# Query norms by matmuls into a column of ones, key scales in another instruction form, and a new order of the engines' work in a fused attention and expert kernel

## The chip, the cores and the metric

The kernel runs on one core of a Trainium2 chip. The metric is the device time of one execution in microseconds; the median of three runs is given, and one further execution was profiled. The engines named below are PE (TensorE; its weight loads have rows of their own, PEld), ACT (ScalarE), DVE (VectorE), POOL (GpSimd) and SP, which issues most transfers. Each has its own stream of instructions, executed in program order, and waits on semaphores of the others.

## The reference, cut to what matters

The whole is a two-layer block: linear attention with a gated delta rule (32 value heads, 16 key heads) beside 64 routed experts, then a small second layer. The change lies in the first layer's attention:

```python
mixed = hidden_states @ w_qkv
y = conv1d(x, conv_w, groups=CONV_DIM)             # 4 taps per channel
mixed = silu(y)
q, k, v = jnp.split(mixed, [KEY_DIM, 2 * KEY_DIM], axis=-1)
q = q / sqrt(sum(q * q, axis=-1) + 1e-6) * DK ** (-0.5)
k = k / sqrt(sum(k * k, axis=-1) + 1e-6)
# over the tokens: S = S * exp(g); delta = (v - k S) * beta; S = S + k^T delta; o = q S
og = o * silu(z)
on = og * rsqrt(mean(og * og) + EPS) * norm_w
out = on.reshape(B, S, VAL_DIM) @ w_out
```

Here the sum of `q * q` over the 128 channels of a head is what the change computes in another way.

## The kernel before, in words

The attention and the experts run together in `heads_and_experts`, in 64 steps g: 16 key heads by four chunks of 128 tokens, for all four batches at once. The chunk of a step is c = g mod 4; c = 0 is the first chunk of a head and c = 3 the last. The work is a pipeline of three steps' depth: step g projects, convolves and squares the keys, queries and values of chunk g, inverts the triangular matrices of chunk g-1, and solves, updates the state and writes the output of chunk g-2. So `state_update`, which is left out in a head's last chunk, is left out in the steps with c = 1. What each engine does in a step is written out by hand in five functions called `step`, one for each engine; this order is what decides who waits.

Keys and queries come out of the convolution with channels on the partitions and tokens along the row. To sum squares over channels, the kernel before turned them on PE (`turn_keys` and `turn_queries`, line 822: four transposes each into a PSUM bank), and ACT squared the turned tile with an accumulated row sum (`squares`, line 1166: four ACTIVATEs and four reads of the accumulator). The turned keys are needed anyway (`keys_copy`, line 1172); the turned queries served the sums alone. The PSUM banks `psF0` and `psF1` are used in turn by 16 places in a fixed order (`PLACES`), even places in one bank and odd ones in the other; a place may be filled when the place two before it has been drained (`slot_free`). Two of these hold for the steps that follow: `EX_IN` (the turned expert input) waits for ACT's `values(g-1, 0)` (line 1189), and `PRODUCTS1` waits for the drain of `QUERIES_T`.

After the queries come `products` on PE (line 844: keys by keys and queries, half 0 and half 1), which DVE scales into `ATP` (`decayed_products`, line 1461). Between the halves stands `state_update(g-2, 0)` (line 962), which waits for POOL's `rho_w` (line 1726), and this for `gated` (line 1743) and DVE's `outputs` (lines 1528 and 1531). DVE's `key_scales` (lines 1440 to 1442) makes from the keys' square sums the scales `sj` that `decayed_products` needs. `conv` is line 1417, `decays` line 1451, `normed` on POOL line 1749, the `join` of the triangular inverse on POOL lines 1710 to 1716, `history` on DVE line 1432 (1434 for a head's first chunk). In steps with c = 3, DVE rounds the next head's weights in three parts (`high_part`, line 574), and POOL computes the remainder of each (`low_part`, line 578) and has `hidden` (line 1757) and `mask` (line 1695) in its queue between them.

## Time and profile before

| what | before |
|---|---|
| median of 3 runs | 2678.14 us (2676.47 to 2680.68) |
| the profiled execution, its own time | 2679.44 us |
| its span, first to last instruction | 2677.7 us |
| mean granted clock of TensorE | 0.958 of full speed |
| PE busy | 2362.6 us (88%) |
| DVE busy | 2326.0 us (87%) |
| ACT busy | 1788.2 us (67%) |
| POOL busy | 1424.9 us (53%) |

A share of busy time is a mean over the span. The 64 steps begin at about 106 us and end near 2300 us; before them stands the setup, behind them the second layer. A row of the timeline gives the start, the duration, the engine, the line of the kernel and what was written and read; in brackets is how long the engine had sat idle before, and whose work ended that.

### The profile page before, as it was taken

How to read it: one execution, taken by the hardware profiler on the slowest of the kernel's cores; microseconds unless marked ns; L12 is line 12 of the kernel's file. 1: busy time of each engine (PE TensorE's matmuls, PEld its weight loads, DVE VectorE, ACT ScalarE, POOL GpSimd, SP SyncE). 2: the span in 40 equal slices, each digit the busy share in tenths (PEclk: the TensorE clock that was granted, in tenths of full speed). 3: DMA queues.
4: the chain of work that ended last, by engine and by line, in shares of the span. 5: the costliest groups of instructions: out<-in, count | busy, mean ns of one | idle time of the engine just before them, and what ended most of it. 6: DMA issues, size and time to landing. Idle time of an engine off the chain costs nothing. (4 is left out here: it accounts for less than half of the span.)

```text
span 2677.7 us, 74015 instructions
## 1 busy us (share of the span) xinstructions
PE 2362.6 (88%) x27695; PEld 1951.4 (73%) x27696; DVE 2326.0 (87%) x5305; ACT 1788.2 (67%) x5621; POOL 1424.9 (53%) x1368
## 2 busy tenths in 40 slices
PE   1477889999999999999999999999999999758998
PEld 1366777888787878787878787878787878635555
DVE  7677888999999999999999999999999998289996
ACT  1356767787878787878787878787877787412121
POOL 2388885555555555555555555555555555266510
PEclk8679899999999999999999999999999999869999
DMA  5232112212222222221222222212122112263311
GB/s 208 89 94 67 41 42 61 57 50 51 55 57 50 57 50 57 49 57 49 57 50 57 50 57 50 57 49 58 49 57 49 46 49 57 64 206 106 104 59 48
DMA packets 244701, 175.39 MB, mean 66 GB/s; under 512 B 152635, under 2 KB 212714, under 8 KB 243160
## 3 DMA queue, kind: packets, MB, share of 16 engines
q1 hardware_dynamic: 221543, 136.89, 19.1%
q0 software_dynamic: 12288, 24.19, 2.9%
q10 hardware_dynamic: 10512, 9.57, 1.1%
q8 instruction: 222, 3.64, 0.6%
q14 instruction: 136, 1.11, 0.1%
HBM read 126.88 MB, written 53.08 MB: 67 GB/s over the span
## 5 line engine op out<-in xcount | busy, mean ns | idle before, releaser
L1417 DVE SCALAR_TENSOR_TENSOR p_y<-p_xr,cw,p_y 128x512 f32<-128x512 f32 x768 | 760.3, 997 | 33.2 <-ACT p_y L1141 14.4
L798 PE MATMUL p_psF<-xnS,w_hl 128*128 128x512 f32 x1536 | 430.6, 416 | 20.4 <-PEq L651 11.1
L798 PEld LDWEIGHTS p_psF<-xnS,w_hl 128*128 128x128 f32 x1536 | 274.4, 192 | 85.9 <-DVE p_ATP L1461 11.4
L1710 POOL TENSOR_TENSOR p_terms<-p_U 64x512 f32<-64x512 f32 x64 | 130.8, 2043 | 335.8 <-DVE p_U L1486 335.7
L1461 DVE SCALAR_TENSOR_TENSOR p_ATP<-p_psF,p_sj,p_E 128x256 f32<-128x256 f32 x512 | 211.0, 477 | 65.8 <-PE p_psF L844 64.2
L1749 POOL TENSOR_TENSOR p_O<-p_OG,p_sm 128x512 f32<-128x512 f32 x128 | 155.7, 1239 | 195.0 <-DVE p_sm L60 171.8
L1743 POOL TENSOR_TENSOR p_OG<-p_O,p_zs 128x512 f32<-128x512 f32 x128 | 162.6, 1271 | 140.5 <-ACT p_ktok L1172 69.3
L979 PE MATMUL p_psO<-p_wout,p_ont 128*128 128x256 f32 x1024 | 235.3, 383 | 0.1
L1712 POOL TENSOR_TENSOR p_terms<-p_terms 64x256 f32<-64x256 f32 (+1 forms) x256 | 220.0, 859 | 20.1
L1138 ACT ACTIVATE p_xr<-p_psF 128x512 f32<-128x512 f32 x256 | 153.4, 599 | 93.6 <-PE p_psF L798 81.8
L813 PEld LDWEIGHTS p_psF<-w_hl,xnS 128*128 128x128 f32 x1536 | 200.1, 189 | 14.3 <-DVE p_ATP L1461 5.1
L979 PEld LDWEIGHTS p_psO<-p_wout,p_ont 128*128 128x128 f32 x1024 | 191.4, 192 | 25.2 <-ACT p_ont L1253 0.8
L1246 ACT ACTIVATE p_O<-p_OG 128x128 f32<-128x128 f32 x512 | 152.4, 308 | 82.4 <-POOL p_OG L1743 81.7
L813 PE MATMUL p_psF<-w_hl,xnS 128*128 128x256 f32 x1536 | 206.0, 284 | 0.0
L1141 ACT ACTIVATE p_y<-p_psF,cw 128x512 f32<-128x512 f32 x256 | 175.0, 684 | 0.8
L1166 ACT ACTIVATE p_y<-p_psF 128x128 f32<-128x128 f32 x512 | 137.1, 300 | 48.2 <-PE p_psF L822 48.2
L822 PE MATMUL p_psF<-ident,p_kq 128*128 128x128 f32 x512 | 86.1, 292 | 93.7 <-ACT p_kq L1151 93.5
L1451 DVE TENSOR_TENSOR_SCAN p_E<-p_ab,p_identr 128x512 f32<-128x512 f32 x128 | 160.6, 1255 | 8.2 <-DMA p_ab<-decays 8.2
L1966 POOL DMA_INDIRECT w_hl<-expert_out,slot_u x96 | 100.8, 1050 | 86.9 <-DVE acc L2211 36.2
L1189 ACT ACTIVATE p_vs<-p_psF,p_vsc 128x128 f32<-128x128 f32 x512 | 146.2, 379 | 0.0
L822 PEld LDWEIGHTS p_psF<-ident,p_kq 128*128 128x128 f32 x512 | 54.8, 143 | 124.1 <-ACT p_kq L1151 124.1
L844 PE MATMUL p_psF<-p_kq 128*128 128x256 f32 x512 | 138.1, 395 | 5.5 <-ACT p_y L1166 5.5
(337 smaller groups left out, 6153.8 us busy)
## 6 DMA issues: line engine op xcount, KB each, us to landing
p_ab<-decays SPq DMA_DIRECT2D x64, 512.0 KB, 5.5
w_raw<-in_w_in SPq DMA_DIRECT2D x16, 768.0 KB, 4.0
p_wgu<-in_w_gu SPq DMA_DIRECT2D x60, 176.0 KB
expert_out<-p_ye ACTq DMA_DIRECT2D x73, 128.0 KB, 1.7
expert_in<-p_zero SPq DMA_DIRECT2D x16, 512.0 KB, 7.5
blocks_out<-p_ATc SPq DMA_DIRECT2D x64, 128.0 KB
p_DTc<-blocks_back SPq DMA_DIRECT2D x64, 128.0 KB
p_xe<-expert_in SPq DMA_DIRECT2D x60, 128.0 KB
```

The source lines that it names most:

```text
L798: m = pe.matmul(b4(psF[f % 2][:, :]), w_hl[:, wp, kt, ty * P:(ty + 1) * P], xnS[:, xp, kt, :].rearrange("p (b t) -> p b t", b=B)[:, :, c * ...
L813: m = pe.matmul(psF[f % 2][:, (b % 2) * 2 * P:(b % 2 + 1) * 2 * P], xnS[:, xp, kt, b * S + c * P:b * S + (c + 1) * P], w_hl[:, wp, kt, 4 * ...
L979: m = pe.matmul(psOO[:, b * D:(b + 1) * D], ont[:, v, b, :], wout[:, v, :], start=(v == 0), stop=(v == 1))
L1138: act.activation(xr[:, ty, :, TAPS - 1:], b4(psF[f % 2][:, :]), ACT.Copy)
L1141: act.activation(y[:, ty, :, :], b4(psF[f % 2][:, :]), ACT.Copy, scale=cw[:, ty, TAPS - 1:TAPS]).then_inc(s["drained"], 1)
L1246: m = act.activation(O1[:, v, b, :], OG[:, v, b, :], ACT.Square, accum_out=so[:, v, b:b + 1])
L1417: m = dve.scalar_tensor_tensor(y[:, ty, :, :], xr[:, ty, :, tap:tap + P], cw[:, ty, tap:tap + 1], y[:, ty, :, :], ALU.mult, ALU.add)
L1451: dve.tensor_tensor_scan(flat(E[:, v, :, :]), flat(ab[:, v, :, :]), flat(identr[:, :, :]), 0.0, ALU.mult, ALU.add).then_inc(s["scan"], 1)
L1461: m = dve.scalar_tensor_tensor(ATP[g % 2][:, v, b, :, :], psF[f % 2][:, (b % 2) * 2 * P:(b % 2 + 1) * 2 * P].rearrange("p (u t) -> p u t", ...
L1712: link(pool.tensor_tensor(terms[:, 0:k, :, :], terms[:, 0:k, :, :], terms[:, k:2 * k, :, :], ALU.add))
L1743: pool.tensor_tensor(OG[:, v, :, :], O1[:, v, :, :], zs[g % 2][:, v, :, :], ALU.mult).then_inc(s["og"], 1)
L1749: pool.tensor_tensor(O1[:, v, :, :], OG[:, v, :, :], over(sm[:, 1, 1 + v, :]), ALU.mult).then_inc(s["on"], 1)
```

## The change

The sums of the queries' squares take another way. ACT squares the queries where they lie (`query_squares`, one ACTIVATE of 128x512 into `y`), PE multiplies each batch's 128x128 squares by a column of ones (`query_norms`, four matmuls with one moving column), and ACT copies the four resulting columns (`query_sums`). The turning of the queries and their four accumulating squares go. In `key_scales` the addition of 1e-6 and the product with the gates become SCALAR_TENSOR_TENSOR instructions; the first now reads a second tensor, `floor`, in place of an immediate. The rest is order: on PE, `EX_IN` goes between the two halves of `within`, and `EX_UP` ahead of `level_y`; on ACT, `silu` of the queries goes ahead of `keys_copy`, and `evacuate(g, 2)` ahead of `inverse_copy`; on DVE, `decays(g, 1)` goes ahead of `pivots`, `history(g-1, 1)` behind `conv(g, 0)`, and `output_weights` and the first part of the next weights between the two last convolutions.

```diff
             @block.vector
-                for t in (xr[:, :, :, 0:TAPS - 1], scratch[:, :], D64X[:, :, :, :], TT[0][:, :, :, :]):
+                for t in (xr[:, :, :, 0:TAPS - 1], D64X[:, :, :, :], TT[0][:, :, :, :]):
                     dve.memset(t, 0.0).then_inc(init, 1)
+                dve.memset(ones[:, :], 1.0).then_inc(init, 1)
+                dve.memset(floor[:, :], 1e-6).then_inc(init, 1)
...
-            def turn_queries(g):
-                wait(pe, "silu", g, 2)
-                turn(g, QUERIES_T, lambda b: kq[g % 2][:, b, Q_, :])
+            def query_norms(g):
+
+                slot_free(g, QUERIES_T)
+                wait(pe, "squared", g, 1)
+                for b in range(B):
+                    m = pe.matmul(psF[QUERIES_T % 2][:, b:b + 1], y[:, 1, b, :], ones[:, :], start=True, stop=True)
+                m.then_inc(s["filled"], 1)
...
@@ PE, step @@
                     within(g - 2, 0)
+                expert(g, EX_IN)
+                if g >= 2:
                     within(g - 2, 1)
-                expert(g, EX_IN)
-                turn_queries(g)
+                query_norms(g)
                 products(g, 0)
...
+                expert(g, EX_UP)
                 if g >= 1:
                     level_y(g - 1, 4)
-                expert(g, EX_UP)
...
@@ ACT @@
-            def squares(g, u):
-
-                p, f = g % 2, (KEYS_T, QUERIES_T)[u]
-                wait_filled(act, g, f)
-                if u == 0:
-                    wait(act, "vsc", g - 2, 1)
+            def key_squares(g):
+
+                wait_filled(act, g, KEYS_T)
+                wait(act, "vsc", g - 2, 1)
                 for b in range(B):
-                    m = act.activation(y[:, u, b, :], psF[f % 2][:, b * P:(b + 1) * P], ACT.Square, accum_out=ss[p][:, u, b:b + 1])
-                m.then_inc(s["drained" if u else "kss"], 1)
+                    m = act.activation(y[:, 0, b, :], psF[KEYS_T % 2][:, b * P:(b + 1) * P], ACT.Square, accum_out=ss[g % 2][:, 0, b:b + 1])
+                m.then_inc(s["kss"], 1)
+
+            def query_squares(g):
+
+                wait(act, "silu", g, 2)
+                act.activation(y[:, 1, :, :], kq[g % 2][:, :, Q_, :], ACT.Square).then_inc(s["squared"], 1)
+
+            def query_sums(g):
+
+                wait_filled(act, g, QUERIES_T)
+                act.activation(ss[g % 2][:, 1, :], psF[QUERIES_T % 2][:, 0:B], ACT.Copy).then_inc(s["drained"], 1)
...
@@ ACT, step @@
                 if g >= 1:
                     values(g - 1, 0)
+                silu(g, 1)
                 keys_copy(g)
-                silu(g, 1)
+                query_squares(g)
                 expert(g, EX_IN)
-                squares(g, 1)
+                query_sums(g)
...
@@ DVE, key_scales @@
-                link(dve.tensor_scalar(sm[:, 0, 0, :], ss[g % 2][:, 0, :], 1e-6, None, ALU.add))
+                link(dve.scalar_tensor_tensor(sm[:, 0, 0, :], ss[g % 2][:, 0, :], 1.0, floor[:, :], ALU.mult, ALU.add))
                 link(dve.reciprocal(n2[:, :], sm[:, 0, 0, :]))
-                dve.tensor_tensor(sj[:, :, :], gates[:, 0, g % NC:NT:NC, h:h + 2], n2[:, :].unsqueeze(2).to_broadcast([P, B, 2]), ALU.mult).then_inc(s["s_ready"], 1)
+                dve.scalar_tensor_tensor(sj[:, :, :], gates[:, 0, g % NC:NT:NC, h:h + 2], 1.0, n2[:, :].unsqueeze(2).to_broadcast([P, B, 2]), ALU.mult, ALU.mult).then_inc(s["s_ready"], 1)
...
@@ DVE, step @@
+                decays(g, 1)
                 if g >= 1:
                     pivots(g - 1)
-                decays(g, 1)
                 conv(g, 0)
+                if g >= 1:
+                    history(g - 1, 1)
                 if g >= 2:
                     level6(g - 2)
                     residual(g - 2, 1)
                 conv(g, 1)
-                if g >= 1:
-                    history(g - 1, 1)
...
-                output_weights(g)
                 rows_decay(g)
                 row_scales(g)
                 conv(g, 3)
+                output_weights(g)
+                next_weights(g, 0)
                 conv(g, 2)
                 if g >= 1:
                     level(g - 1, 4)
                 next_taps(g)
-                next_weights(g, 0)
                 next_weights(g, 1)
```

PE's instructions between the solve and the products, in a step without a state update (c = 1), before (`p_psS` is the solve, `p_psO` the product within the chunk, `p_xe` the expert input, `p_kq` keys and queries):

```order
L943 MATMUL p_psS<-p_vs,p_TT 128x128 x8
L953 MATMUL p_psO<-p_Ws,p_ATP 128x128 x8
L991 MATMUL p_psF<-ident,p_xe 128x128 x2
L822 MATMUL p_psF<-ident,p_kq 128x128 x4
L844 MATMUL p_psF<-p_kq 128x256 x4
```

And of the changed kernel at the same place:

```order
L950 MATMUL p_psS<-p_vs,p_TT 128x128 x8
L960 MATMUL p_psO<-p_Ws,p_ATP 128x128 x4
L998 MATMUL p_psF<-ident,p_xe 128x128 x2
L960 MATMUL p_psO<-p_Ws,p_ATP 128x128 x4
L837 MATMUL p_psF<-p_ones,p_y 128x1 x4
L851 MATMUL p_psF<-p_kq 128x256 x4
```

The four transposes are gone, and four matmuls with one column stand in their place, ahead of the products as the transposes did.

ACT at the same place in the program, from the values of the chunk before to the output's squares, before:

```order
L1189 ACTIVATE p_vs<-p_psF,p_vsc 128x128 x4
L1172 ACTIVATE p_ktok<-p_psF 128x512
L1151 ACTIVATE p_kq<-p_y 128x4x128
L1266 ACTIVATE p_xeT<-p_psF 128x256
L1166 ACTIVATE p_y,p_ss<-p_psF 128x128 x4
L1246 ACTIVATE p_O,p_so<-p_OG 128x128 x8
```

And of the changed kernel:

```order
L1207 ACTIVATE p_vs<-p_psF,p_vsc 128x128 x4
L1161 ACTIVATE p_kq<-p_y 128x4x128
L1190 ACTIVATE p_ktok<-p_psF 128x512
L1180 ACTIVATE p_y<-p_kq 128x512
L1284 ACTIVATE p_xeT<-p_psF 128x256
L1185 ACTIVATE p_ss<-p_psF 128x4
L1264 ACTIVATE p_O,p_so<-p_OG 128x128 x8
```

The queries' squares now stand third, ahead of PE's sums; before they stood behind PE's turning.

DVE at the end of a step with c = 3, where the next head's weights are rounded, before (`p_y` from `p_xr` is the convolution, `w_hl` the rounded weights, `p_St` the state):

```order
L1417 SCALAR_TENSOR_TENSOR p_y<-p_xr,cw,p_y 128x512 x6
L1504 TENSOR_TENSOR p_Dc<-p_Dc,p_psI 128x256
L1505 STREAM_TRANSPOSE p_DTc<-p_Dc 128x256
L1601 COPY cw<-cw_raw 128x16
L574 CAST w_hl<-w_raw 128x2x256 x2
L1551 TENSOR_TENSOR p_St<-p_St,p_psS 128x512 x2
L574 CAST w_hl<-w_raw 128x2x256
L1451 SCALAR_TENSOR_TENSOR p_E<-p_ab,p_identr 128x512
```

And of the changed kernel:

```order
L1435 SCALAR_TENSOR_TENSOR p_y<-p_xr,cw,p_y 128x512 x3
L575 CAST w_hl<-w_raw 128x2x256
L1435 SCALAR_TENSOR_TENSOR p_y<-p_xr,cw,p_y 128x512 x3
L1522 TENSOR_TENSOR p_Dc<-p_Dc,p_psI 128x256
L1523 STREAM_TRANSPOSE p_DTc<-p_Dc 128x256
L1619 COPY cw<-cw_raw 128x16
L575 CAST w_hl<-w_raw 128x2x256
L1569 TENSOR_TENSOR p_St<-p_St,p_psS 128x512 x2
L575 CAST w_hl<-w_raw 128x2x256
L1469 SCALAR_TENSOR_TENSOR p_E<-p_ab,p_identr 128x512
```

The first of the three casts has moved ahead of three taps; the two others keep their places.

## Rows read from the trace of the kernel before

**Rows 1.** The page's busy time and share of the span

```profile
PE 2362.6 (88%) x27695; PEld 1951.4 (73%) x27696; DVE 2326.0 (87%) x5305; ACT 1788.2 (67%) x5621; POOL 1424.9 (53%) x1368
```

**Rows 2.** Window: length, busy and count of PE, PEld, DVE, ACT, POOL; clock; DMA

```profile
650.00:1161.00 511.00, 482.83 (x6422) 414.07 (x6421) 472.26 (x1042) 409.52 (x1312) 274.38 (x264) 1.00 0.22 54
```

**Rows 3.** Who DVE waited for, 300 to 2200 us: total, times, longest

```profile
DVE p_ATP L1461 <- PE p_psF L844: 44.4, 85, 6.5
```

**Rows 4.** Timeline of ACT in a step with c = 1

```profile
1246.16 1.14 ACT L1189 ACTIVATE p_vs<-p_psF,p_vsc 128x128 f32<-128x128 f32 x4
1247.16 0.63 ACT L1172 ACTIVATE p_ktok<-p_psF 128x512 f32<-128x512 f32 x1
1247.63 0.66 ACT L1151 ACTIVATE p_kq<-p_y 128x512 f32<-128x512 f32 x1
1249.04 0.28 ACT L1166 ACTIVATE p_y<-p_psF 128x128 f32<-128x128 f32 x1 [0.47 <-PE p_psF L822]
```

**Rows 5.** Timeline of PE in the same stretch

```profile
1248.35 0.65 PE L822 MATMUL p_psF<-ident,p_kq 128*128 128x128 f32 x4 [0.34 <-ACT p_kq L1151]
1248.84 1.03 PE L844 MATMUL p_psF<-p_kq 128*128 128x256 f32 x4
1251.62 1.65 PE L798 MATMUL p_psF<-xnS,w_hl 128*128 128x512 f32 x6 [0.25 <-DVE p_ATP L1461]
```

**Rows 6.** Timeline of DVE and POOL in the same stretch

```profile
1247.86 1.27 POOL L1743 TENSOR_TENSOR p_OG<-p_O,p_zs 128x512 f32<-128x512 f32 x1 [2.26 <-ACT p_ktok L1172]
1247.95 1.20 DVE L1442 TENSOR_TENSOR p_sj<-gates,p_n 128x8 f32<-128x8 f32 x1
1249.91 3.23 DVE L1461 SCALAR_TENSOR_TENSOR p_ATP<-p_psF,p_sj,p_E 128x256 f32<-128x256 f32 x8 [0.17 <-PE p_psF L844]
```

**Rows 7.** Timeline: sixteen matmuls with eight columns, in the second layer

```profile
2471.13 1.85 PE L2045 MATMUL p_psM<-p_rt,p_xnt 128*128 128x8 f32 x16
```

**Rows 8.** Timeline of PE in steps with c = 2, 3 and 0

```profile
1144.93 1.03 PE L844 MATMUL p_psF<-p_kq 128*128 128x256 f32 x4
1146.14 1.16 PE L962 MATMUL p_psS<-p_Wr,p_ktok 128*128 128x128 f32 x8 [0.18 <-POOL p_Wr L1726]
...
1178.53 1.03 PE L844 MATMUL p_psF<-p_kq 128*128 128x256 f32 x4
1179.87 1.16 PE L962 MATMUL p_psS<-p_Wr,p_ktok 128*128 128x128 f32 x8 [0.31 <-POOL p_Wr L1726]
...
1214.94 1.03 PE L844 MATMUL p_psF<-p_kq 128*128 128x256 f32 x4
1216.47 1.16 PE L962 MATMUL p_psS<-p_Wr,p_ktok 128*128 128x128 f32 x8 [0.50 <-POOL p_Wr L1726]
```

**Rows 9.** Timeline of DVE and POOL at the end of a step with c = 3

```profile
1193.49 1.39 POOL L578 TENSOR_TENSOR w_hl<-w_raw,w_hl 128x512 fp32r<-128x512 f32 x1 [4.84 <-DVE w_hl L574]
...
1194.86 2.63 DVE L574 CAST w_hl<-w_raw 128x512 fp32r<-128x512 f32 x1
1195.26 0.71 POOL L1695 TENSOR_TENSOR p_M<-p_ATc,masks 128x256 f32<-128x256 f32 x1
1195.94 1.26 POOL L578 TENSOR_TENSOR w_hl<-w_raw,w_hl 128x512 fp32r<-128x512 f32 x1
1197.41 1.21 DVE L1451 TENSOR_TENSOR_SCAN p_E<-p_ab,p_identr 128x512 f32<-128x512 f32 x1
```

**Rows 10.** Line 574 alone: count, duration in ns min/median/max, first and last start

```profile
L574 DVE CAST w_hl<-w_raw x45: 406/419/2636, 233.7 to 2132.9; 128x512 fp32r<-128x512 f32 x45
```

**Rows 11.** Timeline of ACT in the step behind the weights, c = 0

```profile
1207.54 0.63 ACT L1151 ACTIVATE p_kq<-p_y 128x512 f32<-128x512 f32 x1 [1.52 <-DVE p_y L1417]
```

**Rows 12.** Timeline: DVE beside POOL

```profile
1142.43 0.29 DVE L1432 COPY p_xr<-p_xr 128x24 f32<-128x24 f32 x1
...
1152.74 1.04 POOL L1749 TENSOR_TENSOR p_O<-p_OG,p_sm 128x512 f32<-128x512 f32 x1 [4.42 <-DVE p_sm L60]
1152.78 1.55 DVE L1417 SCALAR_TENSOR_TENSOR p_y<-p_xr,cw,p_y 128x512 f32<-128x512 f32 x1
```

More of the change, by code:

```diff
@@ L418 @@
 PARTS = [(kt, wp, xp) for kt in range(KT) for wp, xp in ((0, 0), (0, 1), (1, 0))]
-PER = dict(hist=2, silu=2, silu_v0=1, silu_v1=1, kss=1, vsc=1, s_ready=1, scan=2, rho=1, atp=4,
+PER = dict(hist=2, silu=2, squared=1, silu_v0=1, silu_v1=1, kss=1, vsc=1, s_ready=1, scan=2, rho=1, atp=4,
            compact=4, masked=1, halved=2, pivoted=1, joined=1, spread=4, t5=3, tt=1,
@@ L477, in heads_and_experts @@
         n2 = sb("n2", [P, B])
-        scratch = sb("scratch", [P, 1])
+        floor = sb("floor", [P, B])
+        ones = sb("ones", [P, 1])
         vsc = sb("vsc", [P, B])
@@ L653, in _ @@
             def _(dve):
-                for t in (xr[:, :, :, 0:TAPS - 1], scratch[:, :], D64X[:, :, :, :], TT[0][:, :, :, :]):
+                for t in (xr[:, :, :, 0:TAPS - 1], D64X[:, :, :, :], TT[0][:, :, :, :]):
                     dve.memset(t, 0.0).then_inc(init, 1)
+                dve.memset(ones[:, :], 1.0).then_inc(init, 1)
+                dve.memset(floor[:, :], 1e-6).then_inc(init, 1)
                 dve.tensor_copy(identr[:, :, :], ident[:, :].unsqueeze(1).to_broadcast([P, B, P])).then_inc(init, 1)
-                dve.wait_ge(init, 8)
+                dve.wait_ge(init, 9)
             @block.gpsimd
@@ L1138, in evacuate @@
                 act.activation(xr[:, ty, :, TAPS - 1:], b4(psF[f % 2][:, :]), ACT.Copy)
+                if ty == Q_:
+                    wait_filled(act, g - 1, QUERIES_T)
                 if ty >= 2:
@@ L1293, in step @@
                     queries(g - 2, 1)
-                squares(g, 0)
+                key_squares(g)
                 if g >= 2:
@@ L1310, in step @@
                 compact(g)
+                evacuate(g, 2)
                 if g >= 1:
                     inverse_copy(g - 1, 4)
-                evacuate(g, 2)
                 silu_z(g, 1)
-                if g >= 2:
-                    out_turned(g - 2, 0)
                 if g >= 1:
@@ L1319, in step @@
                 if g >= 2:
+                    out_turned(g - 2, 0)
                     out_turned(g - 2, 1)
@@ L1657, in _ @@
             pivots(STEPS - 1)
+            history(STEPS - 1, 1)
             level6(STEPS - 2)
             residual(STEPS - 2, 1)
-            history(STEPS - 1, 1)
             outputs(STEPS - 2, 0)
@@ L1797, in step @@
                 scatter(g, 9)
+                scatter(g, 10)
                 hidden(g)
                 mask(g)
-                scatter(g, 10)
                 scatter(g, 11)
@@ L1803, in step @@
                 scatter(g, 13)
+                scatter(g, 14)
                 next_weights(g, 1)
-                scatter(g, 14)
                 next_weights(g, 2)
```

## The prediction

> **What bounds the kernel now.** I read the page first: PE is busy for 88% of the span and DVE for 87%, ACT for 67%, POOL for 53% [rows 1]. In a window of the settled part they come to 482.83 and 472.26 us of 511, at full clock [rows 2]: two engines near their limit that hand work to each other, so the question is which wait ends last at the place that is changed. The list of waits says that DVE waits most for the products of line 844, 44.4 us in 85 waits [rows 3]. The timeline of one step shows how the work hangs together there (c = 1, 1246 to 1253 us). ACT is continuously at work: values at 1246.16, the keys' copy at 1247.16, silu of the queries at 1247.63, done at 1248.29 [rows 4]. PE turns the queries at 1248.35, 0.06 us behind, having waited 0.34 us, and starts the products at 1248.84 [rows 5]. DVE starts on them at 1249.91, 1.07 us later, having waited 0.17 us [rows 6]. PE's next projection starts at 1251.62, released by DVE, 0.25 us late [rows 5]. So in this stretch the chain ACT, PE, DVE, PE has no slack worth the name; what comes later on it makes the step longer. In the other three kinds of step a state update stands between the halves of the products, and PE waits before it for POOL, 0.18, 0.31 and 0.50 us [rows 8]: this is the slack there.
>
> **The queries' sums.** I count from V, the start of the values on ACT (1246.16 in rows 4). Before: keys' copy at V + 1.00, silu at V + 1.47, done at V + 2.13; turning from V + 2.19 to the products at V + 2.68. After: silu at V + 1.00, the keys' copy 0.52 later at V + 1.52 (the distance from silu to the next ACTIVATE, 1247.63 to 1248.15, which holds for any successor), the squares at V + 2.0 (a copy's distance is 0.47, from rows 4). The trace has no ACTIVATE that squares 128x512; the nearest rows are 0.63 for the copy and 0.66 for silu of the same shape [rows 4], so 0.65, done at V + 2.65, and PE 0.06 behind at V + 2.71. Taking silu out ahead of the keys' copy wins 0.47, and the extra pass loses more.
>
> The four matmuls of one column aren't in the trace either. Turning took 0.49 us for four (1248.35 to 1248.84, rows 5). The nearest row is the second layer's with 128x128 weights and eight columns: sixteen in 1.85 us [rows 7], so about 0.11 each with the tail of the last taken off. An fp32 product of 128 rows makes two such instructions in the trace (a state update with four calls is x8 [rows 8]), so eight, 0.9 us. The other bound is the spacing of the turning itself, 0.49 / 4 = 0.12, for four only if each call made one instruction: 0.5 us. I take 0.9, since rows 7 are the same kind in all but seven columns. The products then start at V + 2.71 + 0.90 = V + 3.61: **0.92 us later** than before.
>
> The Trainium skill (TensorE: Matmul & The Clock Gate, Back-to-back issue gap) puts a matmul of 1 to 64 columns at some 60 cycles, about 25 ns, in isolation. Eight would then be 0.2 us and the products only 0.2 us late. Rows 7 disagree, at 0.11 us with eight columns, and I follow them; the smaller figure is the rule's side of rival B.
>
> What the 0.92 costs in each kind of step. c = 1: products, DVE and the next projection follow without slack, **+0.92** (PE no longer waits between the halves for ACT's four squares, but DVE took both halves without a break, x8 in 3.23 us [rows 6], so that wait was hidden). In the others PE is free for the state update some 0.88 us after the products' start (they take 1.03, of which I give 0.15 to the tail of the last), and the update started when POOL was done:
> - c = 2: 1144.93 + 0.92 + 0.88 = 1146.73 against 1146.14 [rows 8], **+0.59**
> - c = 3: 1178.53 + 1.80 = 1180.33 against 1179.87, **+0.46**
> - c = 0: 1214.94 + 1.80 = 1216.74 against 1216.47, **+0.27**
>
> The second half and the projections follow the update. Together +2.24 us in four steps. `EX_IN` ahead of the second `within` costs nothing: it must wait until the values are drained at V + 1.2, takes 0.2, and 0.9 of `within` ends at V + 2.3, ahead of the squares at V + 2.71; DVE wants it no sooner, since line 1442 holds it until 1249.15 [rows 6]. If the squares came earlier, this would be late next. ACT's four accumulating squares go (from 1249.04 on [rows 4]), but the output's squares behind them start when the sums are copied, at V + 3.9, where they started before.
>
> **The scales' form.** Line 1442 took 1.20 us for eight elements, from 1247.95 to 1249.15, and POOL's `gated` ran from 1247.86 to 1249.13 [rows 6]: DVE stood until POOL was done. Does the other form escape? The convolution is of that form, and beside POOL it takes 1.55 us, ending 0.55 us behind POOL's end at 1153.78 [rows 12]. So it stands as well, and I cost the edit at nothing; bounds: 0 and 1.0 us of DVE. Even the 1.0 would be covered, as DVE then waits for the products, which come 0.92 later. The new first instruction, with its second tensor, ends before POOL starts.
> The Trainium skill (SBUF — State Buffer, Who interferes with whom) says the same against this edit: a DVE instruction with two SBUF inputs contends with a GpSimd one that reads SBUF, and the second to issue blocks fully; by that rule, as by the rows, the form is worth 0.
>
> **The weights, c = 3.** The third cast takes 2.63 us, from 1194.86, where its kind takes 0.42 in the median [rows 9, 10]: POOL has the remainder of the first part, `hidden`, `mask` and the remainder of the second in its queue, back to back until 1197.20, and DVE comes after them. With the first cast ahead of three taps, POOL's first remainder (1.39) runs beside them. I follow both queues: cast 0.42; the first tap; POOL's remainder holds the second tap by 0.75, `hidden` and the like the third by 0.10; that is 1.27 added ahead of `level`. Behind it, the two other parts with the state's sums need 2.9 us more until the scan, which comes at about 1196.35 in place of 1197.41 [rows 9]: **-1.1 us**. Bounds: 0 (each hold only moves to another instruction) and 2.2 (2.63 - 0.42, all of it). The next step, c = 0, can take it: there silu of the keys waited 1.52 us for DVE [rows 11], so up to 1.5 us count and 1.1 do.
>
> **The order's rest.** The scan ahead of `pivots`: the same instructions before `conv(g, 0)`, and POOL's `join` is held by a tap in place of the scan; 0. `history` (0.29 us beside POOL, rows 12) now delays the residual by 0.3 to 0.5 us, where the solve of that half has about that much room; 0, bound +0.4 in three of four steps. `EX_UP`, the copies and `output_weights`: 0, each has work of its engine's own before what waits for it. POOL's queue changes only in the first eight steps, one scatter a step.
>
> **The sum.** +2.24 - 1.1 = +1.1 us for four steps. For the 14 groups from step 8 on, +16 (1.14 x 14). In the first eight steps POOL's scatters stand in the same queue and lead, and I take 0. The profiled execution took 2679.4 us, so 2695.4; it lies 1.3 above the median of the runs shown, so **2694 us**.
>
> **The rivals.** A is the forecast, 2687 to 2702, chance 0.45.
> B: one column is cheap. At 0.5 us for the sums the products are 0.5 late: +0.5, +0.2, 0 and 0, less 1.1, is -0.4 us for four steps: 2672. Against it rows 7. Chance 0.12.
> C: the weights give all of the 2.2 us, the wait of ACT [rows 11] and 0.7 of DVE's own waits behind it: 2.24 - 2.2 is nothing, 2678, no change. For it the 2.63 [rows 9]; against it that POOL's work still has to run beside DVE's. Chance 0.16.
> D, the other side: the late products are absorbed, since PE gets to the projections no later than the wait for POOL allowed, for instance because rho comes late as well in most steps. It decides if the slack of 0.2 to 0.5 us [rows 8] is in truth 0.9 and more; then only the weights count, -1.1 x 14: 2663. Chance 0.12.
> E: `history` behind the first convolution stands behind POOL's `join` and delays solve, V and all behind it by 0.4 in three of four steps: 17 more (1.2 x 14), 2711. Chance 0.15.
>
> Within 0.2% (5.4 us) is what a measurement can't tell from no change. Slower: A and E, 0.60; faster: B and D, 0.24; same: C, 0.16. The range leaves out half of E and most of D: 2667 to 2711. A alone would be 2687 to 2702.
>
> **What would show it.** Right: the products start 3.6 us behind the values in every step; the eight instructions of one column take 0.9; PE waits for POOL before a state update no more; the scales' last instruction still takes 1.2 us; the third cast falls below 1 us; ACT waits 0.4 us or so in c = 0. Wrong: if the sums take under 0.5 us, if four steps together get no longer, or if the scales' product falls to 0.2 us and DVE gets ahead with it.

## The result and the profile after

| | before | after |
|---|---|---|
| median of 5 runs | 2680.57 us (2676.47 to 2682.32) | 2708.86 us (2706.32 to 2712.28) |
| ratio | 1 | 1.0111, 95% interval 1.0099 to 1.0123 |
| profiled execution: its own time, its span | 2679.44, 2677.7 us | 2708.57, 2706.8 us |
| mean granted clock | 0.958 | 0.963 |

The changed kernel is 1.1% slower, 28 us; forecast were 16. The direction and the range held, the size did not: it is nearly twice the forecast one. The page's busy times, beside [rows 1]:

```profile
PE 2387.0 (88%) x27952; PEld 1988.5 (73%) x27952; DVE 2339.8 (86%) x5306; ACT 1737.5 (64%) x5237; POOL 1386.6 (51%) x1368
```

PE works 24 us more, ACT 51 us less. That ACT has less to do brings nothing: what counts is where its new pass stands. The same window as in [rows 2] shows it in the shares:

```profile
650.00:1161.00 511.00, 480.31 (x6309) 416.43 (x6307) 464.81 (x1020) 389.11 (x1208) 263.00 (x262) 1.00 0.21 54
```

PE, DVE, ACT and POOL are all less busy in it, at full clock: each waits more. The list of waits, 300 to 2200 us (engine, line, whom it waited for: total, times, longest), names the place; beside [rows 3]:

```profile
DVE p_ATP L1479 <- PE p_psF L851: 77.0, 59, 2.3
ACT p_ss L1185 <- PE p_psF L837: 52.1, 55, 1.2
PE p_psS L969 <- POOL p_Wr L1744: 0.3, 1, 0.3
```

The last of them before:

```profile
PE p_psS L962 <- POOL p_Wr L1726: 17.3, 38, 4.4
```

DVE waits 77.0 us for the products, in place of 44.4. PE's wait for POOL ahead of the state updates, the slack of [rows 8], is down from 38 waits with 17.3 us to one of 0.3 us in the whole stretch. The timeline of ACT in a step with c = 1 answers to [rows 4]:

```profile
1395.16 1.13 ACT L1207 ACTIVATE p_vs<-p_psF,p_vsc 128x128 f32<-128x128 f32 x4
1396.16 0.66 ACT L1161 ACTIVATE p_kq<-p_y 128x512 f32<-128x512 f32 x1
1396.68 0.62 ACT L1190 ACTIVATE p_ktok<-p_psF 128x512 f32<-128x512 f32 x1
1397.15 0.66 ACT L1180 ACTIVATE p_y<-p_kq 128x512 f32<-128x512 f32 x1
1399.02 0.17 ACT L1185 ACTIVATE p_ss<-p_psF 128x4 f32<-128x4 f32 x1 [0.93 <-PE p_psF L837]
```

And PE's in the same stretch, beside [rows 5]:

```profile
1396.35 0.44 PE L998 MATMUL p_psF<-ident,p_xe 128*128 128x128 f32 x2 [0.46 <-ACT p_vs L1207]
1396.62 1.06 PE L960 MATMUL p_psO<-p_Ws,p_ATP 128*128 128x128 f32 x8
1397.96 1.02 PE L837 MATMUL p_psF<-p_ones,p_y 128*128 128x1 f32 x8 [0.28 <-ACT p_y L1180]
1398.85 1.97 PE L851 MATMUL p_psF<-p_kq 128*128 128x256 f32 x8
```

With V = 1395.16: squares done at V + 2.65, the eight column matmuls from V + 2.80, products from V + 3.69 (forecast 3.61, before 2.68). Both distances hold within 0.01 us in each of the steps 9 to 62. DVE and POOL there, beside [rows 6]:

```profile
1396.93 1.21 DVE L1460 SCALAR_TENSOR_TENSOR p_sj<-gates,p_n 128x8 f32<-128x8 f32 x1
1399.99 2.44 DVE L1479 SCALAR_TENSOR_TENSOR p_ATP<-p_psF,p_sj,p_E 128x256 f32<-128x256 f32 x6 [1.25 <-PE p_psF L851]
...
1396.85 1.27 POOL L1761 TENSOR_TENSOR p_OG<-p_O,p_zs 128x512 f32<-128x512 f32 x1 [1.95 <-DVE p_O L1549]
```

The scales' last instruction still stands until POOL is done, 1.21 us in the new form against 1.20.

ACT in the step behind the weights (c = 0), beside [rows 11], waits 0.97 us for DVE in place of 1.52 (forecast 0.4):

```profile
1492.95 0.63 ACT L1161 ACTIVATE p_kq<-p_y 128x512 f32<-128x512 f32 x1 [0.97 <-DVE p_y L1435]
```

**Step lengths.** Below, a step is measured from the start of its first scan on DVE to that of the next. The row of the scan's line gives the first and the last start of a window; four steps, 36 to 39, before and after:

```profile
L1451 DVE TENSOR_TENSOR_SCAN p_E<-p_ab,p_identr x9: 1201/1206/1396, 1333.1 to 1466.2; 128x512 f32<-128x512 f32 x9
```

```profile
L1469 DVE TENSOR_TENSOR_SCAN p_E<-p_ab,p_identr x9: 1181/1211/1218, 1347.1 to 1482.8; 128x512 f32<-128x512 f32 x9
```

133.1 and 135.7. These and the traces of the experiments give this table: the usual length of each kind of step (the value that most steps from 9 to 62 share within 0.1 us), their sum, and in how many of these 54 steps there is a stretch in which PE's loads of 128 columns take over 0.30 us in place of 0.19, that is, in which the granted clock is at the lower of its levels (1.2 GHz). The two starred lengths contain such a stretch in most steps; without it they are 33.24 and 33.49. The last column is the mean granted clock of all executions of the kernel.

| kernel | c=0 | c=1 | c=2 | c=3 | sum | steps with half clock | ratio to before, 95% | mean clock |
|---|---|---|---|---|---|---|---|---|
| before | 32.1 | 31.7 | 32.6 | 36.7 | 133.1 | 6 | 1 | 0.960 |
| after | 32.5 | 33.8 | 33.5 | 35.9 | 135.6 | 1 | 1.0111 (1.0099 to 1.0123) | 0.961 |
| a_turn | 32.1 | 32.7 | 32.9 | 35.4 | 133.1 | 1 | 0.9967 (0.9954 to 0.9981) | 0.964 |
| b_norms | 32.5 | 32.9 | 34.8* | 37.1 | 137.3 | 18 | 1.0177 (1.0153 to 1.0200) | 0.955 |
| b_weights | 32.1 | 31.7 | 32.6 | 36.2 | 132.6 | 5 | 0.9966 (0.9954 to 0.9979) | 0.962 |
| a_up_back | 32.5 | 32.9 | 35.1* | 36.7 | 137.1 | 8 | 1.0144 (1.0127 to 1.0161) | 0.959 |
| a_half_norms | 32.1 | 33.3 | 33.0 | 35.4 | 133.8 | 0 | 1.0005 (0.9992 to 1.0018) | 0.964 |
| a_turn_pass | 32.1 | 33.1 | 32.9 | 35.5 | 133.6 | 0 | 1.0000 (0.9988 to 1.0012) | 0.965 |
| a_turn_c1 | 32.1 | 31.8 | 33.7 | 35.4 | 133.1 | 0 | 0.9950 (0.9931 to 0.9969) | 0.964 |
| a_in_back | 32.5 | 33.8 | 33.5 | 35.9 | 135.7 | 7 | 1.0147 (1.0129 to 1.0165) | 0.958 |
| b_norms_places | 32.5 | 33.8 | 33.5 | 36.3 | 136.0 | 4 | 1.0149 (1.0127 to 1.0172) | 0.960 |
| b_up | 32.1 | 32.6 | 32.8 | 35.9 | 133.4 | 0 | 1.0006 (0.9996 to 1.0016) | 0.962 |
| b_up_weights | 32.1 | 32.6 | 32.8 | 35.4 | 133.0 | 0 | 0.9977 (0.9965 to 0.9989) | 0.963 |
| a_scales_back | 32.5 | 33.8 | 33.5 | 35.9 | 135.7 | 5 | 1.0110 (1.0089 to 1.0131) | 0.960 |
| a_hist_back | 32.5 | 33.8 | 33.5 | 35.9 | 135.6 | 1 | 1.0099 (1.0076 to 1.0122) | 0.962 |
| a_scan_back | 32.5 | 33.8 | 33.5 | 35.9 | 135.6 | 0 | 1.0133 (1.0117 to 1.0150) | 0.960 |

A name with a_ is the changed kernel with something taken back, one with b_ the kernel before with something of the change. Each ratio is against runs of the kernel before on the same chip, whose median was 2674.7 to 2680.6.

Two things limit what small differences in this table can show. The count of steps with half clock is that of one profiled execution, and it varies: a_scales_back, with the step lengths of the changed kernel, has 5 where that has 1, and the profiled execution of b_norms was the slowest of its four. And of the five kernels with the step lengths of the changed one, after and the last three rows have ratios from 1.0099 to 1.0133 (the fifth, a_in_back, is taken up below), so a difference of 0.2% between two rows, 5 us, tells little.

### The profile page after: what moved, and what is told of

Same layout as the page of the kernel before. It is cut to its first block and busy times, and to the rows that moved or that the text cites. A ratio compares the mean times of both kernels' runs of the same rounds, so it can differ in the third digit from the quotient of the medians.

```text
span 2706.8 us, 74145 instructions
## 1 busy us (share of the span) xinstructions
PE 2387.0 (88%) x27952; PEld 1988.5 (73%) x27952; DVE 2339.8 (86%) x5306; ACT 1737.5 (64%) x5237; POOL 1386.6 (51%) x1368
## 5 line engine op out<-in xcount | busy, mean ns | idle before, releaser
L1435 DVE SCALAR_TENSOR_TENSOR p_y<-p_xr,cw,p_y 128x512 f32<-128x512 f32 x768 | 801.3, 1047 | 38.9 <-ACT p_y L1151 20.7
L1728 POOL TENSOR_TENSOR p_terms<-p_U 64x512 f32<-64x512 f32 x64 | 86.1, 1345 | 425.6 <-DVE p_U L1504 425.6
L986 PE MATMUL p_psO<-p_wout,p_ont 128*128 128x256 f32 x1024 | 242.1, 390 | 0.1
L960 PE MATMUL p_psO<-p_Ws,p_ATP 128*128 128x128 f32 x1024 | 140.1, 281 | 4.7
L960 PEld LDWEIGHTS p_psO<-p_Ws,p_ATP 128*128 128x128 f32 x1024 | 124.2, 192 | 15.5 <-ACT p_Ws L1258 12.8
L1232 ACT ACTIVATE p_D64X<-p_Dc 32x256 f32<-32x256 f32 x128 | 53.2, 416 | 124.6 <-DVE p_DTc L1523 123.0
```

Of the source, the lines that this page charges most:

```text
L960: m = pe.matmul(psO[v][:, b * P:(b + 1) * P], ATP[g % 2][:, v, b, 1, :], Ws[:, v, b, :], start=True, stop=True)
L986: m = pe.matmul(psOO[:, b * D:(b + 1) * D], ont[:, v, b, :], wout[:, v, :], start=(v == 0), stop=(v == 1))
L1435: m = dve.scalar_tensor_tensor(y[:, ty, :, :], xr[:, ty, :, tap:tap + P], cw[:, ty, tap:tap + 1], y[:, ty, :, :], ALU.mult, ALU.add)
```

## The experiments

### The two halves of the change

First I asked whether the loss is the sums' or the order's: the changed kernel with the old sums (a_turn), the kernel before with the new sums and the order as it was (b_norms), and the kernel before with only the first part of the weights moved (b_weights).

```diff
 a_turn, from the changed kernel
-                query_norms(g)
+                turn_queries(g)
...
-                query_squares(g)
                 expert(g, EX_IN)
-                query_sums(g)
+                squares(g, 1)
```

> The changed kernel with the queries' sums as before (turned on PE, four accumulating squares on ACT), all of the new order and the scales' form kept. If the late products (0.9 us behind where they were) are the larger cost, also because they push the last tap into POOL's hidden: the products start 2.7 us behind the values, and the time falls to 2660 to 2672 us. If the order alone costs as much as the sums: about 2690 us. If the order costs all of it: within 4 us of 2709 us.

Measured: 2668.36 us (2666.94 to 2671.65), 0.3% faster than before. The query sums cost the changed kernel 40 us; the rest of the change gains 10 (9 by the ratio).

```diff
 b_norms, from the kernel before
-                keys_copy(g)
                 silu(g, 1)
+                keys_copy(g)
+                query_squares(g)
                 expert(g, EX_IN)
-                squares(g, 1)
+                query_sums(g)
...
-                turn_queries(g)
+                query_norms(g)
```

> The kernel before with the queries' new sums alone (squares on ACT ahead, four one-column matmuls, a copy; silu of the queries ahead of the keys' copy; nothing else of the order, scales in the old form). The prediction's term of 2.24 us for four steps gives 2680 + 34 = 2714 us for 15 groups, less what the first steps absorb: 2704 to 2716 us. If only a collision with POOL made the change slow, this kernel stays under 2695 us; if the late products are absorbed, at 2680.

Measured: 2727.82 us (2718.32 to 2737.06), 49 us slower than before and beyond the range expected. In steps at full clock it is +0.4, +1.2, +0.6 and +0.4, 2.6 us in four, 36 in 14 groups. The rest was not foreseen: in 18 of 54 steps the granted clock falls. The timeline of PE shows one of them, step 38,

```profile
1439.26 0.63 PE L823 MATMUL p_psF<-ident,p_y 128*128 128x128 f32 x4 [0.31 <-ACT p_y L1148]
1441.04 1.09 PE L823 MATMUL p_psF<-ident,p_kq 128*128 128x128 f32 x4 [1.15 <-ACT p_kq L1158]
1441.91 3.20 PE L948 MATMUL p_psS<-p_vs,p_TT 128*128 128x128 f32 x16
```

and by the windows behind the pause (the column behind the five engines is the granted clock):

```profile
1441.00:1444.00 3.00, 2.96 (x14) 2.97 (x15) 2.93 (x4) 1.28 (x9) 2.77 (x4) 0.52 0.00 0
1444.00:1446.00 2.00, 2.00 (x17) 2.00 (x16) 0.49 (x2) 1.31 (x4) 0.45 (x1) 0.87 0.20 23
```

PE waited 1.15 us for silu of the keys and then worked at half clock: the solve took 3.20 us in place of 1.95. A step with c = 2 and such a stretch is 1.6 us longer than one without.

```diff
 b_weights, from the kernel before
                 conv(g, 3)
+                next_weights(g, 0)
                 conv(g, 2)
                 if g >= 1:
                     level(g - 1, 4)
                 next_taps(g)
-                next_weights(g, 0)
```

> The kernel before with one move: the first part of the next head's weights is rounded ahead of the last convolution. By the prediction's term (1.1 us in each of 15 steps with c = 3, all of which the next step can take): 2660 to 2668 us against 2680, and the third cast falls from 2.6 us to under 1. Rival: POOL's work only holds other instructions of DVE, and the time stays at 2680 within 4.

Measured: 2669.52 us (2668.15 to 2670.83), just outside the range expected; c = 3 is shorter by 0.5 us, not 1.1. DVE and POOL in such a step show why:

```profile
1453.05 0.42 DVE L574 CAST w_hl<-w_raw 128x512 fp32r<-128x512 f32 x1
1453.38 3.97 DVE L1417 SCALAR_TENSOR_TENSOR p_y<-p_xr,cw,p_y 128x512 f32<-128x512 f32 x3
...
1459.66 0.53 DVE L574 CAST w_hl<-w_raw 128x512 fp32r<-128x512 f32 x1
```

```profile
1453.55 1.71 POOL L578 TENSOR_TENSOR w_hl<-w_raw,w_hl 128x512 fp32r<-128x512 f32 x1 [1.75 <-DVE w_hl L574]
1455.52 0.60 POOL L1757 TENSOR_TENSOR p_hb<-p_gsb,p_usb 88x128 f32<-88x128 f32 x1 [0.26 <-ACT p_usb L1272]
1456.08 0.72 POOL L1695 TENSOR_TENSOR p_M<-p_ATc,masks 128x256 f32<-128x256 f32 x1
```

The third cast falls from 2.63 to 0.53 us, as said. But the three taps take 3.97 us in place of some 2.25 (three of 0.75): POOL's remainder, `hidden` and `mask` hold them for 1.7, of which the prediction had 0.85. 2.1 less 1.7 is 0.4, near the 0.5 measured.

### Where in the sums the time is

```diff
 a_half_norms, from the changed kernel
-                for b in range(B):
+                for b in (0, 2):
                     m = pe.matmul(psF[QUERIES_T % 2][:, b:b + 1], y[:, 1, b, :], ones[:, :], start=True, stop=True)
...
```

The cut part makes ACT's copy write each of the two sums twice; the kernel leaves out the sums of batches 1 and 3.

> The changed kernel with the product into the column of ones for batches 0 and 2 alone, whose sums then stand for the other two (half of the query sums are left out): four instructions of TensorE less in each step, 0.44 us. Theory (the products hang on the sums without slack in every kind of step, also where a state update stands between the halves): each step gets shorter by 0.44, 1.76 for four, 25 us in all, so about 2684 us beside 2709 of the changed kernel. Rival (in the three kinds of step with a state update the wait for GpSimd takes up the difference, and only c = 1 counts): 0.44 x 14 = 6 us, 2703. Second rival (the ACTIVATE that squares is the whole of the loss): no change.

Measured: 2680.42 us (2677.76 to 2683.26), steps shorter by 0.4, 0.5, 0.5 and 0.4. Each tenth of a microsecond on PE between squares and products counts in every kind of step.

```diff
 a_turn_pass, from a_turn
+                query_squares(g)
                 expert(g, EX_IN)
...
-                wait(pe, "silu", g, 2)
+                wait(pe, "squared", g, 1)
                 turn(g, QUERIES_T, lambda b: kq[g % 2][:, b, Q_, :])
```

> The changed kernel with the turned queries of before (sums from them, as before), but with the ACTIVATE that squares the queries left in behind the keys' copy, and the turning waiting for it: of the path's two parts the extra pass alone, its result unused. Theory (the pass costs where there is no slack, 0.55 us in c = 1 and 0.2 in c = 2, and nothing in the others; TensorE's longer products the rest): 0.75 x 14 = 10 us beyond the turned version, 2678 to 2681 us. Rival (the pass counts in full in every step, 0.5 x 56): 2696.

Measured: 2675.93 us (2671.62 to 2678.39), just under the range expected; four steps 0.5 us longer than a_turn, nearly all of it in c = 1 (+0.4), where no slack stands behind. By ratios it is 9 us (1.0000 less 0.9967). Of the 2.5 us that the sums cost in four steps, the extra ACTIVATE with its wait is 0.5; the larger part comes with PE's eight instructions in place of four.

### The scales' form, and the small moves

```diff
 a_scales_back, from the changed kernel
-                dve.scalar_tensor_tensor(sj[:, :, :], gates[:, 0, g % NC:NT:NC, h:h + 2], 1.0, n2[:, :].unsqueeze(2).to_broadcast([P, B, 2]), ALU.mult, ALU.mult)
+                dve.tensor_tensor(sj[:, :, :], gates[:, 0, g % NC:NT:NC, h:h + 2], n2[:, :].unsqueeze(2).to_broadcast([P, B, 2]), ALU.mult)
```

> The changed kernel with the key scales in the form of before. Theory (the form is worth nothing, since the last instruction ends with GpSimd's in either form): within 0.1% of the changed kernel, 2706 to 2712 us. Rival (the new first instruction is longer and delays the outputs by 0.05 us or so): 1 to 3 us faster.

Measured: 2708.85 us (2706.81 to 2714.11), and the last instruction takes 1.20 us in the median in place of 1.21: the form is worth nothing.

```diff
 a_hist_back, from the changed kernel
-                if g >= 1:
-                    history(g - 1, 1)
                 if g >= 2:
                     level6(g - 2)
                     residual(g - 2, 1)
                 conv(g, 1)
+                if g >= 1:
+                    history(g - 1, 1)
```

> The changed kernel with the second history behind the second convolution again. Theory (it has room where it stands): 2706 to 2712 us, no change. Rival (beside GpSimd's join it takes 0.3 to 0.4 us and stands ahead of the residual, and the solve of that half and all behind it come later by that): 0.2 to 0.4 us in three of four steps, 8 to 17 us faster, 2692 to 2701.

Measured: 2706.05 us (2699.36 to 2714.49), ratio 1.0099 (1.0076 to 1.0122). The interval holds the changed kernel's ratio; step lengths are the same within 0.05. Rival E of the prediction is out.

```diff
 a_scan_back, from the changed kernel
-                decays(g, 1)
                 if g >= 1:
                     pivots(g - 1)
+                decays(g, 1)
                 conv(g, 0)
```

> The changed kernel with pivots ahead of the second scan again. Theory: GpSimd's join then starts 1.1 us sooner and holds the taps of the first convolution less, silu of the keys and the turned keys come 0.1 to 0.3 us sooner: 0 to 0.5 us for four steps, up to 7 us faster, 2702 to 2709. Rival (the prediction's: the same instructions, no change): 2706 to 2712. Second rival: join takes its hold at another place, the pause of TensorE ahead of solve in c = 2 grows again beyond 1.1 us and the granted clock falls in some steps, 2 to 10 us slower.

Measured: 2709.75 us (2708.57 to 2711.20), the profiled span 2706.8 as after, and the same step lengths: no change. Its ratio, 1.0133, is the highest of the four kernels with these lengths.

### EX_UP ahead of level_y

In c = 1 the last two taps of the changed kernel have this row, and POOL this timeline:

```profile
L1435 DVE SCALAR_TENSOR_TENSOR p_y<-p_xr,cw,p_y x2: 752/1200/1648, 1410.2 to 1411.0; 128x512 f32<-128x512 f32 x2
```

```profile
1410.98 0.45 POOL L1775 TENSOR_TENSOR p_hb<-p_gsb,p_usb 88x128 f32<-88x128 f32 x1 [2.79 <-ACT p_usb L1290]
1411.39 0.72 POOL L1713 TENSOR_TENSOR p_M<-p_ATc,masks 128x256 f32<-128x256 f32 x1
```

The last tap takes 1.65 us in place of 0.75. `EX_UP` comes earlier on PE, so `hidden` and `mask` get onto POOL 34 ns ahead of the last tap; with `EX_UP` back, in a_up_back and a_turn_c1, `hidden` starts 0.64 and 0.66 us behind this tap, and the tap takes 0.75. I took this for the missing cost of c = 1 (2.1 us longer, forecast 0.9).

```diff
 a_up_back, from the changed kernel
-                expert(g, EX_UP)
                 if g >= 1:
                     level_y(g - 1, 4)
+                expert(g, EX_UP)
```

> The changed kernel with one move undone: on PE the expert's up product stands behind level_y again. Theory 1 (the move lets POOL's hidden and mask get the port ahead of the last convolution tap, which then takes 1.65 us in place of 0.75 in steps with c = 1 and 2, and delays level): the tap falls to 0.75 us there and the time falls by 12 to 25 us, to some 2685 to 2697 us. Theory 2 (PE sets the length of these steps, the tap only fills DVE's slack): the tap falls as well, but the time stays within 4 us of the changed kernel's 2709 us.

Measured: 2715.33 us (2712.51 to 2717.08), 6 us slower by the medians. My theory fell. c = 1 did get 0.9 us shorter, but at the end of it PE is 0.85 us further behind the scan, and c = 3 is longer by it; the sum at full clock is 135.5 (32.5 + 32.9 + 33.5 + 36.7), as after. And in 8 of the 14 steps with c = 2 the clock fell, 1.6 us each. The same move back in c = 1 alone, with the old sums:

```diff
 a_turn_c1, from a_turn
+                if g % NC != 1:
                     expert(g, EX_UP)
                 if g >= 1:
                     level_y(g - 1, 4)
+                if g % NC == 1:
+                    expert(g, EX_UP)
```

> The changed kernel with the turned queries of before, and EX_UP behind level_y again in the steps of c = 1 alone. Theory: EX_UP ahead of level_y lets GpSimd run hidden and mask beside the last tap, which stretches that tap from 0.75 to 1.65 us in c = 1, where VectorE is the engine that arrives last; back in its place there, c = 1 takes 31.8 in place of 32.74 us, the other kinds of step stay (32.1, 32.85, 35.4): 2668 - 13 = 2655 us. Rival: as in the whole undoing of that move the next step, c = 2, starts with TensorE 0.85 us behind, and gives the 0.9 back, with a fall of the granted clock in some steps: 2668 to 2672.

Measured: 2665.46 us (2662.35 to 2669.34). c = 1 is 0.9 shorter and c = 2 0.8 longer, as the rival had it. So the tap's 0.9 us are not on the path: what goes over from c = 1 to c = 2 is PE's work, then ACT's `evacuate`, then DVE's first convolution, and DVE waits 0.74 us for ACT there in the changed kernel (in a_turn_c1 it doesn't wait there):

```profile
1419.20 0.28 DVE L1504 TENSOR_REDUCE p_U<-p_terms 64x32 f32<-64x128 f32 x1
1420.22 3.04 DVE L1435 SCALAR_TENSOR_TENSOR p_y<-p_xr,cw,p_y 128x512 f32<-128x512 f32 x3 [0.74 <-ACT p_y L1151]
```

The other way round, `EX_UP` moved in the kernel before, alone and with the weights:

```diff
 b_up and b_up_weights, from the kernel before
+                expert(g, EX_UP)
                 if g >= 1:
                     level_y(g - 1, 4)
-                expert(g, EX_UP)
```

> The kernel before with EX_UP ahead of level_y, and nothing else. Theory: the last tap in c = 1 gets 0.9 us longer beside hidden and mask, but the next step gives it back, since TensorE's chain is what goes over from step to step: four steps take 133.1 us as before, 2676 to 2681 us; if the pauses of TensorE in c = 0 and c = 2 get shorter by it, the stretches at half the clock go and it is 2668 to 2674. Rival (the longer tap is on the path): 0.9 x 14, 2690 us.

> The kernel before with EX_UP ahead of level_y and the first part of the weights ahead of the last convolution; the old path of the queries' sums. Theory (the weights win 0.5 us in four steps, EX_UP keeps the granted clock up in c = 2): four steps 132.9 us without a fall of the clock, 2662 to 2668 us, as fast as the fastest so far. Rival (EX_UP takes back what the weights give, by the tap that it makes longer): 2672 to 2676.

Measured: 2676.15 us (2672.58 to 2682.78) and 2670.69 us (2664.07 to 2673.69). Four steps get 0.3 us longer at full clock, and no step of the profiled execution is left with half clock: together nothing. With the weights, 133.0, 0.2% faster than before; the ratio, 0.9977, lies between the theory's time and the rival's. These two moves alone thus give the step lengths of a_turn within 0.2 us; the other moves of the order, those of ACT and of `output_weights` among them, add nothing that shows in a sum of four steps.

### EX_IN between the halves of within

With the old sums, then with the new ones:

```diff
 a_turn_in (from a_turn) and a_in_back (from the changed kernel)
                     within(g - 2, 0)
-                expert(g, EX_IN)
-                if g >= 2:
                     within(g - 2, 1)
+                expert(g, EX_IN)
```

> The changed kernel with the turned queries of before, and EX_IN behind both halves of within again. Theory: where the queries are turned, the second half of within ends 0.17 us after silu of the queries, so the turning waits for it; EX_IN back in its place lets it start 0.12 to 0.16 us sooner in each step, 0.5 us in four, 7 us in all: 2661 us. Rival (the waits for GpSimd ahead of the state updates take it up, only c = 1 counts): 2 us, 2666 to 2668.

> The changed kernel with EX_IN behind both halves of within again, all else as it is. Theory (the squares of the queries end later than the second half of within, so EX_IN is covered): 2706 to 2712 us, no change. Rival (ACT's copy of EX_IN then stands ahead of the sums and delays them): 1 to 5 us slower.

Measured: 2666.27 us (2661.94 to 2668.52), ratio 0.9966 as a_turn: the step lengths stay (32.1, 32.7, 32.9, 35.4), and the 7 us of the theory don't come. And 2713.42 us (2711.07 to 2717.07), ratio 1.0147, by the median 4.6 us over the changed kernel, against my theory. Beside a_scan_back, measured with it, it is 3.7 us, and the intervals of the ratios overlap (1.0129 to 1.0165, 1.0117 to 1.0150): that it is slower at all is likely and not shown. The usual steps are the same to 0.05 us; if there is a difference it is the clock, low in 7 steps of the profiled execution. Step 50 on PE, and the windows:

```profile
1837.92 0.38 PE L998 MATMUL p_psF<-ident,p_xe 128*128 128x128 f32 x2
1839.37 1.02 PE L837 MATMUL p_psF<-p_ones,p_y 128*128 128x1 f32 x8 [1.07 <-ACT p_y L1179]
1840.26 1.93 PE L851 MATMUL p_psF<-p_kq 128*128 128x256 f32 x4
```

```profile
1837.00:1840.50 3.50, 2.43 (x21) 2.22 (x20) 2.74 (x5) 2.57 (x8) 2.36 (x4) 0.98 0.18 19
1840.50:1843.50 3.00, 3.00 (x12) 2.64 (x12) 1.27 (x4) 2.05 (x14) 2.14 (x2) 0.50 0.42 137
```

Behind `within` as a whole PE waits 1.07 us in one piece for the squares. With `EX_IN` in between it waits twice, 0.46 and 0.28 us in the rows of PE after, above, and 0.56 and 0.28 in a step of the kind of step 50, c = 2:

```profile
1428.16 0.44 PE L998 MATMUL p_psF<-ident,p_xe 128*128 128x128 f32 x2 [0.56 <-ACT p_vs L1207]
1429.78 1.02 PE L837 MATMUL p_psF<-p_ones,p_y 128*128 128x1 f32 x8 [0.28 <-ACT p_y L1180]
```

To see whether these two places are what the new order gives, I put them alone into b_norms:

```diff
 b_norms_places, from b_norms
                     within(g - 2, 0)
+                expert(g, EX_IN)
+                if g >= 2:
                     within(g - 2, 1)
-                expert(g, EX_IN)
...
+                expert(g, EX_UP)
                 if g >= 1:
                     level_y(g - 1, 4)
-                expert(g, EX_UP)
```

> The kernel before with the new path of the queries' sums, and beside it only two places of the new order: EX_IN between the halves of within, EX_UP ahead of level_y. Theory (the path alone cost 48 us, 36 of it as work on the chain and the rest as half-clock stretches behind pauses of TensorE of 1.3 to 1.7 us in c = 0 and c = 2; the two places break these pauses up): the stretches are gone in the settled part, four steps take 135.7 to 136.1 us, 2711 to 2716 in all, in place of 2728. Rival (the stretches come from the later products alone): 2724 to 2730, no change.

Measured: 2716.85 us (2713.85 to 2719.21), ratio 1.0149 (1.0127 to 1.0172) against 1.0177 (1.0153 to 1.0200); the intervals overlap. Steps with half clock went from 18 to 4 (expected: none), though the usual four steps got 0.3 us longer, and the mean clock of all executions rose from 0.955 to 0.960. PE's pause in c = 2 is the one before the turned keys:

```profile
1427.20 0.66 PE L823 MATMUL p_psF<-ident,p_kq 128*128 128x128 f32 x4 [0.83 <-ACT p_kq L1159]
1427.69 1.95 PE L948 MATMUL p_psS<-p_vs,p_TT 128*128 128x128 f32 x16
```

0.83 us in place of 1.15, and the solve back at 1.95. But the pause alone doesn't decide it. The kernel before has the pause of 1.15 us too, and its clock falls in 3 of 14 steps with c = 2, where that of b_norms falls in 12. a_turn_c1 waits 1.41 us at this place in most steps and keeps its clock. And a_up_back waits 1.41 us there in every such step: in step 38 the solve then takes 3.25 us, in step 42 of the same execution 1.95:

```profile
1423.25 1.03 PE L825 MATMUL p_psF<-ident,p_kq 128*128 128x128 f32 x4 [1.41 <-ACT p_kq L1161]
1424.08 3.25 PE L950 MATMUL p_psS<-p_vs,p_TT 128*128 128x128 f32 x16
...
1560.41 0.65 PE L825 MATMUL p_psF<-ident,p_kq 128*128 128x128 f32 x4 [1.41 <-ACT p_kq L1161]
1560.91 1.95 PE L950 MATMUL p_psS<-p_vs,p_TT 128*128 128x128 f32 x16
```

What else is wanted stays open.

## Why the prediction was right and wrong

**The bottleneck and the chain: right.** The products come 1.01 us later behind the values (3.69 less 2.68, forecast 0.92), the eight instructions take 0.89 (0.9), and PE's waits for POOL are gone. The Trainium skill (TensorE: Matmul & The Clock Gate, Back-to-back issue gap), by whose figure for an isolated matmul eight would take an estimated 0.2 us, is not borne out by this form: 0.11 us each here.

**The step that failed is the size of the sum, +1.1 us for four steps.** At full clock it is +2.5 (135.6 less 133.1). Its two terms were both mis-sized, the weights by more.

**The weights, -1.1 us: the larger miss.** Alone they give -0.5, since POOL's queue holds the taps for 1.7 us, not 0.85. `EX_UP`, costed at nothing, takes 0.3 of it back (b_up, b_up_weights). In ordinary steps the whole new order brings nothing (a_turn 133.1, before 133.1), where the sum had -15.4 us. By the medians it brings 10.

**The queries' sums, +2.24 us in four steps.** Measured as after less a_turn it is 0.4, 1.1, 0.6 and 0.4, 2.5 us in four steps at full clock, so each kind of step gave 0 to 0.2 more than forecast. c = 1 has +0.09 from PE starting 0.15 behind ACT in place of 0.06, and +0.07 from DVE starting 1.14 behind the products in place of 1.07. Over the kernel it is 40 us by the medians where the term gave 31. The profiled spans are 36.9 apart (2706.8 less 2669.9): 32.7 of it lies between the scans of steps 9 and 63, and 4.7 ahead of step 9, where the prediction had put nothing. Of the parts, the extra pass measured 0.5 us in four steps; its 0.52, less the slacks that the prediction gives each kind of step, would be 0.77.

**The clock was no term of the sum, and the range held by luck.** At full clock the 54 steps from 9 to 62 take 36 us more than before; on top of the profiled 2679.4 that is some 2715, beyond the range's 2711. The two profiled executions are only 29 apart, because that of before has half clock in 6 of these steps, which cost 1.2 to 1.4 us each and one of them 2.4, and that of after in 1, at 1.6. Over all executions the mean granted clocks of the two are the same (0.960 and 0.961), so this advantage of the changed kernel is not shown to be a lasting one, and with the same steps the ratio was up to 1.0133.

What the order brings by the medians, 10 us, is in part the clock: 0.964 in a_turn beside 0.960 in before over all executions. Between the profiled ones (7.8 us apart) 3.5 us lie in steps 9 to 62, where a_turn has 1 step with half clock in place of 6, and 4.7 ahead of step 9. I had costed `EX_IN` and `EX_UP` at nothing, naming covers for their own time; I had not asked what they do to PE's pauses. Taken back from the changed kernel, the first gives 2713 and the second 2715, in place of 2709. Single executions of kernels with the step lengths of the changed one reached 2714.5, so that these two moves keep it at 2709 is likely and not shown. And the sums in the old order cost 49 us in place of 40.

The account in medians: forecast +31 - 15 = +16; measured +40 - 10 = +30 (28 in the direct comparison).

**The form, the scan, history: 0, as said**, by a run for each. For the form the timeline shows it too. The Trainium skill (SBUF — State Buffer, Who interferes with whom), which spoke against the edit, agrees with the trace: 1.21 us in the new form beside POOL, 1.20 in the old.

**The signs named** came: the products' place, the 0.9, the third cast (none of the changed kernel's 45 casts takes over 0.53). ACT's wait in c = 0 is 0.97 and not 0.4, which is the weights' missing half seen from the other side. Rivals B to E are out: the column isn't cheap, the weights give less than forecast, the late products aren't absorbed, and `history` costs nothing.

**The fastest version** is a_turn_c1, 2665.5 us, 0.5% under before: the old sums with the new order. It beats a_turn (0.9967) by less than the intervals tell.

## What to carry to other kernels

Moving a reduction from one engine to another is priced by where its steps stand on the chain between engines, not by the busy time it frees: ACT got 51 us of work less, and the kernel lost 28. It gave up four transposes (0.49 us on PE) for eight matmuls with one column (0.89) and one more hand-over between engines.
When an instruction is moved, ask what it does to the pauses of TensorE as well as to the path; two moves that leave the sum of four steps at full clock as it was, or 0.3 us longer, went with 4 to 11 us by the medians and with a different granted clock. These differences are near what equal kernels show here, so the advice is to look, not a rule. A step measured from one engine's mark to the next can get shorter without the kernel getting faster: sum over a whole period.

## What was not expected of the hardware

- The granted clock fell to about half (0.52, 0.50 in windows of 3 us) for some 3 us behind PE's pauses of 1.07 and 1.15 us, in the middle of stretches in which PE was busy for over nine tenths of the time. It fell in every second group of four steps in a_in_back (steps 10 to 50), though the same pause of 1.07 us stands in each, and it costs 1.6 us a time. Behind a pause of 1.41 us it fell in 8 of 14 steps of a_up_back.
- VectorE's tap beside GpSimd's short instructions: where they start 34 ns ahead of it, it takes 1.65 us; where they start 0.64 us behind it, 0.75.
- A matmul with one moving column takes as long as one with eight: 0.11 us each in a row of eight (0.89), [rows 7] had the same.
